# Attention counts in two half banks, stages around the edge loop pipelined, first edge records loaded early

## What is computed

```python
# layer 0, for each of 8 relations: attention over edges and self loops
e = leaky_relu(s[src] + d[dst]); w = exp(e - segment_max(e, dst)[dst])
out += segment_sum((w / denom[dst])[:, None] * h[src], dst) + br
# layer 1: out_deg = segment_sum(1, src); neighbour sums, two weights
# layer 2: three message layers, relu(neighbour_sum(x) @ W_msg + x @ W_self + b)
# layer 3: edge MLP, mean over the edges of a source node, node MLP
h   = relu(relu(concat(x[dst], edge_attr) @ W1.T + b1) @ W2.T + b2)
agg = segment_sum(h, src) / max(out_deg, 1)
out = relu(concat(x, agg, u) @ Wa.T + ba) @ Wb.T + bb
```

## Time and profile before

| | us |
|---|---|
| median of the three runs | 4038.57 |
| the profiled execution's own time | 4019.43 |
| its span, first to last instruction | 4017.7 |
| attention: first to last maximum on VectorE (122 batches) | 211.1 to 1820.8 |
| ln2, edge tables and the way to the edge loop's first add | 2316.9 to 2405.2 |
| the edge loop's adds on GpSimd | 2405.2 to 3924.0 |
| node update, ln3 and the output | 3924.0 to 4017.7 |

### The profile page before, as it was taken

The page is one execution under the profiler, slowest core; times in us unless marked ns, Lnnn a source line. Parts: engine busy times, 40 slices in busy tenths (PEclk is TensorE's granted clock), DMA queues, the critical chain, the costliest instruction groups (busy, mean ns, idle before and its releaser), DMA issues. The chain is left out here.

```text
span 4017.7 us, 77702 instructions
## 1 busy us (share of the span) xinstructions
PE 2872.7 (72%) x16134; PEld 2016.3 (50%) x16135; DVE 2334.3 (58%) x8562; ACT 1464.6 (36%) x3326; POOL 2316.7 (58%) x1835
## 2 busy tenths in 40 slices
PE   7167777767777676655879949788777877788752
PEld 4045555555555555442434436666666656566531
DVE  6288888888888888765342244444444444444423
ACT  1055455445554555432000014334333333333320
POOL 0276666666666666540000008888888888888880
PEclk8555555565555555556989969898888988988876
DMA  3433433433343334882532315555555555555543
GB/s 126 98 105 100 119 106 102 113 106 106 98 118 106 97 106 116 75 123 94 173 100 75 99 19 57 54 53 54 53 54 54 52 53 54 54 52 54 54 41 78
DMA packets 651839, 336.53 MB, mean 84 GB/s; under 512 B 436752, under 2 KB 612163, under 8 KB 650820
## 3 DMA queue, kind: packets, MB, share of 16 engines
q0 software_dynamic: 148736, 86.57, 22.4%
q1 hardware_dynamic: 443062, 112.07, 13.5%
q10 hardware_dynamic: 59856, 136.11, 8.9%
HBM read 156.42 MB, written 202.84 MB: 89 GB/s over the span
## 5 line engine op out<-in xcount | busy, mean ns | idle before, releaser
L2110 POOL DMA_INDIRECT sums<-el_rows,el_idx x816 | 1270.2, 1557 | 648.1 <-DVE el_rows L2324 399.7
L811 POOL DMA_INDIRECT at_hs<-table,at_rec_s x976 | 1038.8, 1064 | 605.0 <-issue 284.9
L952 PE MATMUL near_ps<-at_pair_hot,at_src_low_hot 128*128 128x425 f16 x976 | 503.4, 516 | 468.8 <-ACT at_count_s L849 293.9
L849 ACT CAST at_count_s<-near_ps 128x400 f16<-128x400 f32 x976 | 482.5, 494 | 887.9 <-PE near_ps L952 379.1
L2322 DVE CAST el_idx<-el_place 128x4 uint32<-128x4 f32 x204 | 35.4, 173 | 844.0 <-DMA sums<-el_rows,el_idx 802.0
L924 PEld LDWEIGHTS sums_ps<-at_hw,at_hit 128*128 128x128 f32 x1952 | 471.5, 333 | 34.4 <-issue 28.9
L924 PE MATMUL sums_ps<-at_hw,at_hit 128*128 128x66 f32 x1952 | 442.5, 408 | 8.3 <-DVE acc L998 8.3
L952 PEld LDWEIGHTS near_ps<-at_pair_hot,at_src_low_hot 128*128 128x128 f16 x976 | 128.1, 131 | 608.2 <-ACT at_count_s L849 355.2
L990 DVE TENSOR_SCALAR at_pair_hot<-iota_wide,at_rec_s 128x400 f16<-128x400 f16 x976 | 322.8, 333 | 1.5
L2258 ACT ACTIVATE el_h<-el_h_ps,el_valid 128x128 f32<-128x128 f32 x816 | 233.2, 368 | 240.8 <-PE el_h_ps L2172 169.6
L2126 PE MATMUL el_miss_t<-ident_b,el_miss 128*128 128x128 bf16 x816 | 84.9, 266 | 311.8 <-DVE el_miss L2296 311.8
(11 more groups left out here) (355 smaller groups left out, 5134.3 us busy)
## 6 DMA issues: line engine op xcount, KB each, us to landing
slots<-at_count_s ACTq DMA_DIRECT2D x122, 850.0 KB
el_rec<-attr SPq DMA_DIRECT2D x816, 32.0 KB
chunk<-slots SPq DMA_DIRECT2D x240, 100.0 KB
attr<-in_edge_attr SPq DMA_DIRECT2D x19, 1248.0 KB
chunk<-slots ACTq DMA_DIRECT2D x224, 100.0 KB
at_rec_s<-meta SPq DMA_DIRECT2D x992, 3.5 KB
at_hs<-table,at_rec_s POOLq DMA_INDIRECT x976
el_pair<-meta SPq DMA_DIRECT2D x816, 1.0 KB
```

The source lines that it names most:

```text
L811: pool.indirect_dma_start(hs[:, s, u, :], None, k.table, bass.IndirectOffsetOnAxis(rec[:, s, u, 0:1].bitcast(U32), 0)).then_inc(gathered[s ...
L849: a.copy(count[:, (n.o + d) % 2, i, 0:AW], near[:, (n.o + d) % 2, 0:AW]).then_inc(count_ready, 1)
L952: pe.matmul(near[:, s, 0:SW], low_hot[:, s, i, :], pair_hot[:, s, i, :], start=False, stop=True, skip_group_check=(i > 0)).then_inc(near_r ...
L2110: pool.indirect_dma_start(k.sums_flat[a], bass.IndirectOffsetOnAxis(idx[:, j, a:a + 1], 0), rows[:, j, a, :], None, compute_op=ALU.add).th ...
```

## The change

Three parts, in the diff's order.

- **`attention`.** The 425 columns of a visit are cut into 208 (`LW`) and 217, one half in each bank of `near`. Each visit now has two count matmuls and two copies (208 and 192 columns), each half with its own pair of semaphores; the carries become four matmuls. The 25 degree columns are copied to SBUF by ScalarE once per batch, and VectorE adds them from there.
- **`ln2` and `edge_tables` become one stage.** The small loads start at its head, `visit_row` first, and behind it SyncE loads the records of the edge loop's first two batches. Turning and multiplying alternate bank by bank; ScalarE copies the turned columns and makes the first two bf16 parts, VectorE the remainder and the third, and the bias parts are spread between them.
- **`node_update` and `ln3` become one stage** over three groups of tiles (8, 8, 9). SyncE and ScalarE issue two of the four tables each, group by group; the weights stand behind the first group. The engines' lists alternate between the groups; ScalarE takes over the copies from PSUM; normalization and output go group by group.

```diff
+LW = AW // 32 * 16 + 16
@@ attention, ACT
-                a.copy(count[:, (n.o + d) % 2, i, 0:AW], near[:, (n.o + d) % 2, 0:AW]).then_inc(count_ready, 1)
+                act.wait_ge(left_ready, n(B, d * B + i + 1))
+                a.copy(count[:, s, i, 0:LW], near[:, 0, 0:LW]).then_inc(left_copied, 1)
+                act.wait_ge(near_ready, n(B, d * B + i + 1))
+                a.copy(count[:, s, i, LW:AW], near[:, 1, 0:AW - LW]).then_inc(count_ready, 1)
+            def degrees(n, d):
+                if n.after(2 - d):
+                    act.wait_ge(deg_added, n(1, d - 1))
+                a.copy(deg[:, (n.o + d) % 2], near[:, 1, AW - LW:SW - LW]).then_inc(deg_copied, 1)
@@ attention, PE
+                for h, (c0, c1) in enumerate(((0, LW), (LW, SW))):
+                    if n.after(1 - d):
+                        pe.wait_ge(count_ready if h else left_copied, n(B, d * B))
+                        if h:
+                            pe.wait_ge(deg_copied, n(1, d))
...
+                    for i in range(2):
+                        pe.matmul(near[:, h, 0:c1 - c0], k.carry_by[:, i, :],
+                                  rows[:, bass.ds(at[i], 1), c0:c1].rearrange("p i c -> p (i c)"), start=(i == 0), stop=False)
...
+                    pe.wait_ge(left_copied, n(B, d * B + i))
+                pe.matmul(near[:, 0, 0:LW], low_hot[:, s, i, :], pair_hot[:, s, i, 0:LW], start=False,
+                          stop=True, skip_group_check=(i > 0)).then_inc(left_ready, 1)
+                if i:
                     pe.wait_ge(count_ready, n(B, d * B + i))
-                pe.matmul(near[:, s, 0:SW], low_hot[:, s, i, :], pair_hot[:, s, i, :], start=False,
+                pe.matmul(near[:, 1, 0:SW - LW], low_hot[:, s, i, :], pair_hot[:, s, i, LW:SW], start=False,
                           stop=True, skip_group_check=(i > 0)).then_inc(near_ready, 1)
@@ edge_tables, SP
+            sp.dma_start(k.visit_row[:], ...).then_inc(row_loaded, 16)
...
+            sp.wait_ge(row_loaded, 16)
+            for s in range(2):
+                load_records(nc, k, sp, s * B, s)
@@ edge_tables, PE (turn(q): transposes of 4 tiles; product(q): matmuls with w1a)
+            turn(0)
+            for q in range(DC):
+                if q + 1 < DC:
+                    turn(q + 1)
+                product(q)
@@ edge_tables, DVE
+            for q in range(DC):
+                if q >= 2:
+                    dve.wait_ge(y_done, q - 1)
+                remainder(q)
+                if q < 4:
+                    step(v.tensor_copy(k.b2_parts[:, q], b2_sum[:]))
+                if q == 4:
+                    step(v.memset(k.ones_b[:], 1.0))
+                if q:
+                    third(q - 1)
+            third(DC - 1)
@@ node_update
+        T = ((0, 8), (8, 16), (16, NT))
@@ SP
+            load_sums(sp, 0, (0, 1))
+            for dst, src in ((wa_u, k.wa_u), (u0, k.u0), (ba, k.ba), (wa_x, k.wa_x)):
+                sp.dma_start(dst[:], src).then_inc(w_loaded, 16)
+            load_sums(sp, 1, (0, 1))
+            load_sums(sp, 2, (0, 1))
+            for g, (t0, t1) in enumerate(T):
+                sp.wait_ge(normed, g + 1)
...
@@ PE
+            turn(0)
+            hidden(0)
+            turn(1)
+            outer(0)
+            hidden(1)
+            turn(2)
+            turn_back(0)
+            outer(1)
+            hidden(2)
+            turn_back(1)
+            outer(2)
+            turn_back(2)
@@ DVE
+            means(0)
...
+            means(1)
+            means(2)
+            centre(0)
+            centre(1)
+            norm(0)
+            centre(2)
+            norm(1)
+            norm(2)
```

More of the change, by code:

```diff
@@ new lines, in product @@
+            def product(q):
+                pe.wait_ge(x_copied, q + 1)
+                if q == 0:
+                    pe.wait_ge(w1a_loaded, 16)
+                t0, t1 = tiles(q)
+                for t in range(t0, t1):
+                    m = pe.matmul(ps[:, q, (t % 4) * H:(t % 4 + 1) * H], k.x_t[:, t * P:(t + 1) * P], w1a[:], start=True,
+                                  stop=True)
+                m.then_inc(y_ready, 1)
+            turn(0)
[3 more added lines that the diff above has]
+                product(q)
@@ L2385, in _, with turn, hidden @@
         @block.tensor
         def _(pe):
+            def turn(g):
+                pe.wait_ge(mean_ready, g + 1)
+                for q in chunks(g):
+                    for t in range(4 * q, min(4 * q + 4, NT)):
+                        m = pe.transpose(ps[:, q, (t % 4) * P:(t % 4 + 1) * P], part[:, 0, t, :], k.ident[:])
+                    m.then_inc(turned, 1)
+            def hidden(g):
+                for q in chunks(g):
+                    pe.wait_ge(mean_copied, q + 1)
+                    pe.matmul(ps[:, q, 0:cols[q]], wa_x[:], k.x_t[:, q * CW:q * CW + cols[q]], start=True, stop=False)
+                    pe.matmul(ps[:, q, 0:cols[q]], wa_m[:], mean_t[:, q * CW:q * CW + cols[q]], start=False,
+                              stop=True).then_inc(z_ready, 1)
@@ new lines, in outer, with turn_back @@
+            def outer(g):
+                for q in chunks(g):
+                    pe.wait_ge(z_done, q + 1)
+                    pe.matmul(ps[0:D, q, 0:cols[q]], wb[:], z[:, q * CW:q * CW + cols[q]], start=True,
+                              stop=True).then_inc(o_ready, 1)
+            def turn_back(g):
+                for q in chunks(g):
+                    pe.wait_ge(o_done, q + 1)
+                    for t in range(4 * q, min(4 * q + 4, NT)):
+                        m = pe.transpose(ps[:, q, (t % 4) * D:(t % 4 + 1) * D], o_t[:, t * P:(t + 1) * P], k.ident[0:D, 0:D])
+                    m.then_inc(back, 1)
@@ L2398, in _ @@
-            for q in range(DC):
-                pe.wait_ge(z_done, q + 1)
-                pe.matmul(ps[0:D, q, 0:cols[q]], wb[:], z[:, q * CW:q * CW + cols[q]], start=True,
-                          stop=True).then_inc(o_ready, 1)
-            pe.wait_ge(o_done, DC)
-            turn_columns(pe, k, ps, o_t, D, back)
+            turn(0)
[6 more added lines that the diff above has]
+            outer(1)
@@ L2417, in _ @@
+            means(0)
+            act.wait_ge(ba_ready, 1)
+            relu(0)
+            means(1)
+            outputs(0)
+            relu(1)
+            means(2)
+            outputs(1)
+            relu(2)
+            outputs(2)
+            for g in range(G):
+                deviation(g)
         @block.vector
```

285 lines of the change are left out of this document (180 added, 105 removed).

## The result

The change runs in 4018.14 us, median of five runs (4011.25 to 4025.07), against 4039.75 for the kernel before (five runs, 4037.94 to 4045.41): a ratio of 0.9946, interval 0.9930 to 0.9961. That is 21.6 us or 0.54% faster. The forecast was 3929, with a range of 3880 to 3990: the sign was right, the size four to five times too large, and the time lies outside the range.

The account below looks back on a forecast made before the run. GpSimd was taken to bound the edge loop, the count matmul and copy chain much of attention's step. Attention 45, front 34 and tail 31 sum to 110 us: 4038.6 - 110 = 3929, range 3880 to 3990.

Parts of the forecast that it names:

- The seams: The new stages before and after the edge loop: forecast to gain 34 and 31 us, 65 together, range 50 to 76.
- Front: Stage before the edge loop: normalization's end to first add 45 us in place of 79, gain 34, bounds 25 to 40.
- the second round of `src_t`: TensorE before the edge loop: would come 8 to 9 us behind the first mask instead of 14.2, gaining about 6.
- Tail: Last add to the end: 62 us in place of 94, means under the loads, gain 31, bounds 20 to 36.
- the 15%: Tail's table loads: if 15% slower in pieces, the last third lands 3 to 4 us later, the gain shrinking as much.
- attention's 45 us: Counts in two halves in attention: 0.37 us a batch over 122 batches, 45 us gained; bounds 153 gained to 30 slower.
- What bounds the kernel now: Opening section: GpSimd bounds the edge loop; no engine is full in attention, where VectorE idles 153.0 us before its maximum.
- the chain of count matmul and copy: Attention: TensorE count matmul, ScalarE copy, next matmul sets much of the 13.30 us step, at 1.12 us a visit.
- Rival B: VectorE's work plus stops already fill an attention batch, so only the stages around the edge loop gain: 3974, chance 0.26.
- I take these stops as given: Attention: 78 unexplained ScalarE waits, 233.1 us, assumed to stay; a shorter chain only lets engines catch up sooner.
- Rival D: Attention: half copies make ScalarE the pace setter, costing 150 us; total 85 slower at 4124, chance 0.05.
- E: Attention's halves move as one and gain nothing, the stages around the edge loop gain half: 4006, chance 0.05.

Follow-up runs that it names:

- seams_only: Kernel before with both new stages around the edge loop, attention unchanged (no half banks): 3863.80 us against 3926.04, ratio 0.9849, on a chip without stops.
- act_halves: Kernel before with each visit's copy in two halves, one count matmul waiting for both: 3932.39 us against 3926.04; again 3938.06 against 3926.92; chips without stops.
- turns12: Kernel before with both new stages, whole counts, and twelve batches per attention loop turn instead of six: 3959.93 us, ratio 0.9853, chip with stops.
- turns12_split: The full change, counts in halves, with twelve batches per attention loop turn instead of six: 4002.45 us, ratio 0.9950 to the kernel before, chip with stops.
- padded: Kernel before with both new stages and 96 always-fulfilled waits at the end of TensorE's attention list: 3958.41 us, one run, chip with stops.

## Why the prediction was wrong

**The seams were right, the front by luck in part.** Front: forecast 34, measured 34.0 in the two profiles; from the first transpose to the first add 45.0 us (2396.84 to 2441.8) in place of 78.9, forecast 45 for 79. Inside, two terms were too good. A bank costs TensorE 3.0 us (2401.68 to 2404.68), not 2.6, since each switch between transposes and products adds 0.14 to 0.30 us to matmuls that otherwise start 0.21 apart; so the first mask comes 22.6 us after the first transpose and not 20. And the second round of `src_t` comes 11.1 us behind the first mask (2419.43 to 2430.55), not 8 to 9. What made up for these 5 us was not in the forecast: from that round to the first add it takes 11.3 us in place of 16.6, with TensorE's granted clock at 0.86 in place of 0.56, mostly the 2.4 GHz level in place of mostly 1.2 (windows before and with the change, columns as in the earlier trace rows):

```profile
2388.60:2405.20 16.60, 16.57 (x79) 11.52 (x80) 5.39 (x27) 3.90 (x10) 0.00 (x0) 0.56 0.14 22
...
2430.50:2441.80 11.30, 11.30 (x83) 8.41 (x81) 5.47 (x27) 5.19 (x12) 0.04 (x1) 0.86 0.18 28
```

Tail: forecast 31, measured 30.2, the thirds landing at 10.4 and 25.4 us where I had 9.5 and 25. None of the 15% shows that I had allowed for loads in pieces. They were my estimate, made on account of the rule of the Trainium skill ("DMA: Bandwidth & Descriptors", section "Measured", batch to at least 1 MiB), which rests on loads issued from GpSimd. Here twelve loads of 0.5 MB on two queues bring 6.55 MB in 25.4 us, so in this trace the smaller loads cost nothing that shows. Together 64.2 in the profiles, 62.2 and 64.5 by the medians on chips without stops, forecast 65.

**The step that failed is the first term of the sum, attention's 45 us,** and in it the assumption under "What bounds the kernel now": that the chain of count matmul and copy "sets much of the step". The parts of the chain were sized well enough (copies 0.339 and 0.334 us, carries 0.47 after the last copy, 0.17 us less at the change of batch against 0.20). But I put all of the 153 us that VectorE idled before its maximum down to masks between the count copies, though the earlier trace rows has 102.3 of them as "issue". By the view of the tile in the kernel before, the mask ended only a third:

```profile
  issue: 102.3, 39
  ACT at_hit_t L831: 49.7, 21
```

What the runs showed in place of the chain is two sources. One is VectorE's wait for its own code at the loop's turn: 16 waits, 68.6 us in seams_only, and 45.1 us at the same 16 batches in the trace of before, 2.6 to 2.9 at most of them. The other is the stops. Where there are none, VectorE is 92% busy, most of the rest stands at the turns, and the split is worth 0.05% or nothing. For the chips without stops that is Rival B, which I gave 0.26, with 3974 as its time; on the chip of the forecast the split cost time, which B does not have.

**The second failure is "I take these stops as given".** They are not given: with the split, and so with two handovers from TensorE to ScalarE per visit in place of one, 202 to 206 copies were stopped in place of 154 to 165, and VectorE idles 52 to 67 us more before its maximum (210.4 - 158.6 in the pair with twelve batches a turn, 219.8 - 153.0 in the first). On such a chip the split costs 42.5 us, which eats two thirds of the seams; 64 - 43 = 21, the 21.6 measured. Which part of the split brings the added stops (the second matmul, the second copy, the wider set of semaphores) was tried only on chips without stops and stays open. Rival D had the right sign for attention, by another mechanism (ScalarE's room): act_halves, which adds the same two copies, costs 6 to 11 us on chips without stops, so ScalarE's load alone does not bring 42; with stops it was not tried.

**The range** failed with it: on the slow side it ended at B with its seams short by 15, and between that and D at 4124 no case stood in which the seams gain and attention loses some of it, which is what came. E's 4006 lies nearest to the 4018 measured, but by chance: its seams gain half and its attention loses nothing, where the seams gained in full.

## What to carry to other kernels

Before costing a shorter chain, take the idle time of the engine that should profit apart by place: if it comes in a few long pieces at the loop's turn, look for instruction packets in the DMA records; if it comes behind waits that nothing in the program ends, the chain is not what it waits for. Where engines are stopped for no reason that the program shows, measure before you split a handover: here the split came with 22 to 31% more stops, though why is open. If a change has independent parts, run each alone: here the two seams without the split are as fast as the whole on one kind of chip and about 43 us faster on the other (there by turns12 and turns12_split). The best version in hand is `seams_only`, though it was itself not run on a chip with stops; padded, which is it with 96 waits more, took 3958.41 there.

## What the runs showed of the hardware

- The kernel before takes 3914 to 3937 us on three chips, 4010 to 4028 on a fourth and 4038 to 4045 in its first runs (4019 when profiled). With whole counts attention takes 1510 to 1524 us where there are no stops and 1610 to 1614 where there are; the rest of the program is the same within 10. A change in attention can't be judged from one of the two kinds.
- VectorE stands still for 2.6 to 4.7 us at the loop's turn, with its inputs ready, and goes on about 2.0 us after the start of an instruction packet. The stores of `count` put that packet off by up to 2 us in the middle of attention (0.6 to 0.95 us after VectorE has run out without them, up to 2.7 with them).
- In a stop TensorE's signal is late (139 of 157), and ScalarE starts within 0.1 us of it. Traces with stops lack over a third of the semaphore updates.
- 96 fulfilled waits on TensorE in one stage made a later one 6.7 us longer; 2.9 of these are one wait that ends 2.8 us after the start of an instruction packet of 16 KB.
- In seams_only the last 19 steps take 14.7 us on average (279.8 / 19), the middle ones 12.3. Most of them take 11.4 to 13.1; five take 15 to 34 (from batches 107, 108, 113, 114 and 117). The transfer queue of the gathers is busy for 13.2% of 16 engines' time from 1300 to 1420 and for 67.0% from 1560 to 1680, with fewer packets:

```profile
q0 software_dynamic: 2464, 2.61, 13.2%
...
q0 software_dynamic: 1837, 1.95, 67.0%
```

Why the last batches' gathers take so long was not tried.
